# First attention of a hybrid network: group maxima taken a group ahead, a third stack buffer, and work laid out in pairs of slots

## The reference

```python
xn = (xg - mean) * jax.lax.rsqrt(var + EPS)
xn = xn.reshape(b, c, n) * norm_w[None, :, None] + norm_b[None, :, None]
qkv = jnp.einsum('oc,bcn->bon', qkv_w, xn) + qkv_b[None, :, None]
q, k, v = jnp.split(qkv, 3, axis=1)
...
attn = jnp.einsum('bhdn,bhdm->bhnm', q * scale, k * scale)
attn = jax.nn.softmax(attn, axis=-1)
out = jnp.einsum('bhnm,bhdm->bhdn', attn, v).reshape(b, c, n)
out = jnp.einsum('oc,bcn->bon', proj_w, out) + proj_b[None, :, None]
return out.reshape(b, c, h, w) + x_in
```

## Time and profile before

| | |
|---|---|
| median of 3 runs | 5458.73 us (5458.4 to 5465.98) |
| profiled execution | 5458.14 us, its span 5456.3 us |
| busy in the span | PE 4884.0 us (90%), DVE 3601.6 (66%), ACT 2986.6 (55%), POOL 1018.5 (19%) |
| mean granted clock of TensorE | 0.949 of 2.4 GHz |
| attention | from the start to about 2078 us |

### The profile page before, as it was taken

One profiled execution on the slowest core, in us unless ns is written; L12 is line 12 of the kernel. 1 busy time (PEld: TensorE's weight loads), 2 busy tenths in 40 slices (PEclk: granted clock), 3 DMA queues, 4 the chain that ended last, 5 costly groups with the idle time before them and its releaser, 6 DMA issues.

```text
span 5456.3 us, 90109 instructions
## 1 busy us (share of the span) xinstructions
PE 4884.0 (90%) x29729; PEld 2693.7 (49%) x29729; DVE 3601.6 (66%) x7699; ACT 2986.6 (55%) x5452; POOL 1018.5 (19%) x1348
## 2 busy tenths in 40 slices
PE   5999999999999988868888888889899999999999
PEld 1222222232222222247777777778755555555554
DVE  6777777777777744555656656555676766766765
ACT  2666666666666663315555555556655455555552
POOL 2221122232121222112333333333200000000000
PEclk7999999999999998879999999999999999999999
DMA  2522222232222211305454545454311111111112
GB/s 85 148 78 88 71 71 81 74 94 84 71 93 72 68 45 28 72 32 154 144 163 142 164 139 165 139 156 115 111 44 48 53 44 51 50 42 51 51 46 74
DMA packets 406330, 477.63 MB, mean 88 GB/s; under 512 B 87640, under 2 KB 249648, under 8 KB 403760
## 3 DMA queue, kind: packets, MB, share of 16 engines
q1 hardware_dynamic: 372128, 424.84, 25.8%
q0 software_dynamic: 20576, 35.55, 2.4%
q10 hardware_dynamic: 13168, 11.48, 0.8%
HBM read 308.54 MB, written 145.57 MB: 83 GB/s over the span
## 4 chain that ended last, share of the span: by engine, by line
PE 34%; DVE 16%; issue 3%; DVEq 3%; ACT 2%; ACTq 0%; SPq 0%; DMA 0%
PE n_ps_f L2157 4%; PE n_ps_f L2150 4%; PE n_ps_xy L1805 3%; PE n_ps_h L1795 3%; PE n_ps_c L2197 2%; PE n_ps_h L2209 2%; PE n_ps_f L2144 2%; PE n_ps_f L1653 2%; PE n_ps_xy L2213 1%; DVE n_stats L975 1%; PE n_ps_f L999 1%; DVE n_xln L987 1%; PE n_ps_h L2213 1%; DVEq L2029 1%; DVE n_down_weights L2028 1%
## 5 line engine op out<-in xcount | busy, mean ns | idle before, releaser
L600 ACT ACTIVATE a_probs<-ps_b 128x512 f32<-128x512 f32 x2048 | 1111.0, 594 | 734.9 <-PE ps_b L696 725.1
L456 DVE TENSOR_REDUCE a_negmax<-ps_a 128x1 f32<-128x1024 f32 x1024 | 1219.7, 1221 | 309.6 <-PE ps_a L640 301.1
L696 PE MATMUL ps_b<-a_q_stack,a_k_stack 99*128 99x512 bf16 x2048 | 651.7, 391 | 56.9 <-DMA a_q_stack<-a_shift 49.3
L640 PE MATMUL ps_a<-a_k_stack,a_q_stack 96*128 96x512 bf16 x2048 | 624.9, 403 | 74.3 <-DMA a_k_stack<-split_scratch 64.4
L710 PE MATMUL ps_o<-a_probs,a_v_ones 128*32 128x256 f32 x8192 | 670.5, 400 | 0.0
L1608 ACT ACTIVATE n_hidden<-n_ps_h,n_b 128x128 f32<-128x128 f32 x1472 | 419.3, 373 | 343.6 <-PE n_ps_h L1795 342.3
L1805 PE MATMUL n_ps_xy<-n_down_weights,n_hidden 128*128 x2944 | 409.7, 284 | 80.4 <-ACT n_xy L1622 74.2
L1805 PEld LDWEIGHTS n_ps_xy<-n_down_weights,n_hidden 128*128 128x128 f32 x2944 | 368.5, 196 | 118.2 <-issue 114.6
L2094 ACT ACTIVATE n_down_weights<-n_ps_h 128x512 f32<-128x512 f32 x288 | 172.1, 598 | 428.6 <-PE n_ps_h L2209 323.0
L1795 PE MATMUL n_ps_h<-n_xy,n_up_weights 128*128 128x128 f32 x2944 | 400.9, 280 | 4.5 <-issue 2.4
L696 PEld LDWEIGHTS ps_b<-a_q_stack,a_k_stack 99*128 99x128 bf16 x2048 | 201.0, 100 | 382.1 <-ACT a_probs L600 98.8
(11 more groups left out here) (346 smaller groups left out, 7655.8 us busy)
## 6 DMA issues: line engine op xcount, KB each, us to landing
n_up_weights<-in_L_ffn_W_dram SPq DMA_DIRECT2D x368, 256.0 KB
n_up_weights<-score_scratch SPq DMA_DIRECT2D x512, 128.0 KB, 2.9
split_scratch<-a_pieces SPq DMA_DIRECT2D x180, 256.0 KB
a_q_stack<-split_scratch SPq DMA_DIRECT2D x128, 192.0 KB, 3.6
a_k_stack<-split_scratch SPq DMA_DIRECT2D x128, 192.0 KB, 4.1
rows_scratch<-n_zero SPq DMA_DIRECT2D x16, 1472.0 KB, 10.0
outs_scratch<-n_xy SPq DMA_DIRECT2D x176, 128.0 KB, 2.0
n_xg<-rows_scratch SPq DMA_DIRECT2D x80, 256.0 KB, 3.2
```

What stands on the lines that cost most here:

```text
L456: dve.tensor_reduce(negmax[:, b, t:t + 1], bank, axis=AX.X, op=ALU.max, negate=True).then_inc(ring_read, 1)
L600: act.activation(probs[:, m % PROBS, 512 * k:512 * k + 512], ps_b[:, k, :], ACT.Exp).then_inc(b_exp, 1)
L640: last = pe.matmul(bank[:, cols], q_stack[0:KS, h, 128 * t:128 * t + 128], k_stack[0:KS, h, cols], start=True, stop=True)
L696: pe.matmul(ps_b[:, k, :], k_stack[:, h, 128 * t:128 * t + 128], q_stack[:, h, 512 * k:512 * k + 512], start=True, stop=True).then_inc(b_u ...
```

## The change

- **Order within pairs.** PE handles slots in pairs. In an even slot: shifted scores, then a half weighing of 512 columns. In an odd slot: shifted scores, then the ring entries, among them both maxima of the pair. Before, each slot had ring entries, shifted scores and a quarter weighing of 256 columns.
- **Maxima ahead.** Every pair has two maxima and no pair is without; the list runs 4 maxima further ahead of its group (`EARLIER`). The prologue computes these 4 more. The shifts come at slots 13, 29, 45, 61.
- **Third stack buffer.** The stacks of a group rotate over three places; the third lies in the part of `u_cols` that belongs to the last four images. These images' `u` goes to a DRAM scratch and is loaded back in three parts when the convolution begins.
- **Smaller parts.** Each piece of the maxima is sent as soon as it is ready; `project` is cut in two halves around the shifted scores of slot 31; ACT does its `take` and `qk` steps after the exponentials of the odd slot. The other steps move by some slots.

```diff
+        def stacks(i, g):
+
+            n = (G * i + g) % STACKS
+            return q_stacks[n], k_stacks[n]
...
         def normed():
 
-            work = [(0, ("moments",)), (1, ("sums", 0)), (1, ("norm",))]
-            return work + [(4, ("qk", 0)), (6, ("qk", 1)), (9, ("v",))]
+            work = [(1, ("moments",)), (3, ("sums", 0)), (3, ("norm",))]
+            return work + [(7, ("qk", 0)), (9, ("qk", 1)), (11, ("v",))]
 
         def projected():
 
-            return [(2, ("take", 1, 0)), (4, ("take", 1, 1)), (8, ("recip",)), (29, ("project",)), (30, ("moments2",)),
-                    (31, ("sums", 1)), (32, ("norm2",)), (34, ("turn2",))]
+            return [(1, ("take", 1, 0)), (3, ("take", 1, 1)), (10, ("recip",)), (30, ("project",)), (31, ("project_rest",)),
+                    (31, ("moments2",)), (35, ("sums", 1)), (35, ("norm2",)), (37, ("turn2",))]
 
         def maxima(ahead, g):
 
-            work = [(3 + n * 26 // QUAD, ("scores", ahead, g, n)) for n in range(QUAD)]
-            return work + [(18, ("shift", ahead, g, 0)), (30, ("shift", ahead, g, 1))]
+            return [("scores", ahead, g, n) for n in range(QUAD)]
+
+        EARLIER = 4
+
+        def all_maxima(front):
+
+            work = [(n // 2 * 2 + 1, w) for n, w in enumerate(maxima(0, 1)[EARLIER:])]
+            work += [(13, ("shift", 0, 1, 0)), (29, ("shift", 0, 1, 1))]
+            if front:
+                work += [(QUAD - EARLIER + n // 2 * 2 + 1, w) for n, w in enumerate(maxima(1, 0) + maxima(1, 1)[:EARLIER])]
+                work += [(45, ("shift", 1, 0, 0)), (61, ("shift", 1, 0, 1))]
+            return work
...
+                if G * i + g >= STACKS:
+                    sp.wait_ge(b_up, (G * i + g - STACKS + 1) * (2 * QUAD))
...
                     store_split(0, i + 1)
                     store_split(1, i + 1)
+                    load_stack(i + 1, 0)
                 send_shift(i, 1, 0)
                 send_shift(i, 1, 1)
                 if front:
-                    sp.wait_ge(b_up, i * (2 * SLOTS) + 2 * QUAD)
-                    load_stack(i + 1, 0)
+                    load_stack(i + 1, 1)
...
                 for m, works in enumerate(bodies[kind]):
+                    shifted_scores(i, m)
+                    if m % 2 == 0:
+                        if m >= J:
+                            weigh_values(i, m // J - 1, m % J // 2)
+                        elif kind != "first":
+                            weigh_values(i - 1, G * NT - 1, m % J // 2)
                     n = run(works, kind, i, n, table)
-                    shifted_scores(i, m)
-                    if m >= J:
-                        weigh_values(i, m // J - 1, m % J)
-                    elif kind != "first":
-                        weigh_values(i - 1, G * NT - 1, m % J)
...
+            for n, up in enumerate(late_in):
+                part = slice(PARTS[n], PARTS[n + 1])
+                sp.dma_start(u_cols[:, B - LATE:B, part, :].rearrange("p a c h -> p a (c h)"),
+                             u_dram[:, :, part, :].rearrange("a p c h -> p a (c h)")).then_inc(up, 16)
```

More of the change, by code:

```diff
@@ L192, in plan @@
         def plan(front, back):
             by_slot = [[] for _ in range(SLOTS)]
-            for s, work in (projected() if back else []) + (normed() if front else []) + maxima(0, 1):
+            for s, work in (projected() if back else []) + (normed() if front else []):
                 by_slot[s].append(work)
             for k in range(HALVES):
[L198 to L201, removed]
+                by_slot[QUAD + 1 + 2 * k].append(("take", 0, k))
@@ L202, in plan @@
+            for s, work in all_maxima(front):
+                by_slot[s].append(work)
             return by_slot
         RING = ("scores", "shift", "project", "sums", "qk", "v")
+        PE_ONLY = ("project_rest",)
         BY_ACT = ("qk",)
         ACT_WORK = BY_ACT + ("take",)
-        first = [work for _, work in normed()] + [("split",), ("rows",)] + [work for _, work in sorted(maxima(0, 0), key=lambda x: x[0])]
+        first = [work for _, work in normed()] + [("split",), ("rows",)] + maxima(0, 0)[:QUAD // 2] + [("shift", 0, 0, 0)] + maxima(0, 0)[QUAD // 2:]
@@ L208, in attention_phase @@
+        first += maxima(0, 1)[:EARLIER // 2] + [("shift", 0, 0, 1)] + maxima(0, 1)[EARLIER // 2:EARLIER]
         bodies = {"first": plan(True, False), "middle": plan(True, True), "last": plan(False, True)}
@@ L629, in _, with project_half @@
         def _(pe):
+            def project_half(bank, k):
+                cols = slice(512 * k, 512 * k + 512)
+                for g in range(G):
+                    last = pe.matmul(bank[:, cols], wproj[:, g, :], o_sums[:, g, cols], start=(g == 0), stop=(g == G - 1))
+                return last
             def step(work, i, nxt, prev, parity):
@@ L646, in step @@
                     pe.wait_ge(on_up, prev + 1)
-                    for k in range(HALVES):
-                        cols = slice(512 * k, 512 * k + 512)
-                        for g in range(G):
-                            last = pe.matmul(bank[:, cols], wproj[:, g, :], o_sums[:, g, cols], start=(g == 0), stop=(g == G - 1))
+                    project_half(bank, 0)
+                    return
+                elif what == "project_rest":
+                    last = project_half(bank, 1)
                 elif what == "sums":
@@ L685, in run @@
                         n += 1
+                    elif work[0] in PE_ONLY:
+                        step(work, i, nxt, i - 1 if kind != "closing" else B - 1, (odd + n - 1) % 2)
                 return n
```

98 lines of the change are left out of this document (54 added, 44 removed).

## The result

The changed kernel takes **5493.1 us** in the median of 5 runs (5484.35 to 5495.06), beside 5458.4 for the kernel before on the same chip: ratio **1.0061, 95% interval 1.0046 to 1.0075**. It is slower by more than the 0.2% that can be told from no change, and inside the predicted range; the predicted 5516 was 23 us too high. The profiled execution has a span of 5491.3 us, 35.0 more than the one of before.

A forecast was written before the change was run, and what follows sets the result against it. PE's instruction list was taken to set the pace. A middle image summed to 127.3 us against 122.5; 14 of them gave +67, the ends -10, so +57 on 5458.1: 5516 us, range 5410 to 5580.

The forecast's parts named there:

- PE's list without DVE waits: Middle image: 32 pairs of 2.86 us, 10.0 for other entries, 0.8 waiting for ACT; 102.3 us.
- shifts as third entries: Odd slots: a shift behind two maxima waits 1.1 us for a free bank; 4.3 us for four shifts.
- `qk`, `v` as third entries: Odd slots: the second maxima wait until ACT has read the bank; two `qk` and `v` lose 3.0 us.
- DVE at the image's start: Slots 63 to 5: PE's maxima wait while DVE does `moments`, `sums` and `norm`; 6.1 us lost.
- DVE behind `project`: Up to slot 39: PE's maxima wait while DVE does `moments2`, `norm2` and `turn2`; 8.6 us lost.
- work at the lower clock: Behind the idle at image start and `project`, PE's work runs at half speed: 1.5 us each, 3 an image.
- The pair: Two undisturbed slots: 2.86 us against 3.08 before, with a 512-column weighing of 1.01; ACT barely follows.
- The third rival: The wide weighing brings nothing, 1.14 us for 512 columns: 4.2 us an image, 5575 us; chance 0.05.
- rival 2: The lower clock at both places and the pairs behind costs 7 us an image instead of 3: 5572 us; chance 0.10.
- The DMA waits: PE's two waits at the image's start, 2.0 us, and later ones vanish; the next stacks' load stays hidden before slot 32.
- the ends: Prologue and first image 0, last image -9.5 and -4, convolution's first matmul 3 us later; together -10 us.
- Rival 1: Faster: clock holds (-3), PE's long entries absorb DVE's blocks and third entries (-4 an image): 5418 us; chance 0.22.

The follow-up runs named there:

- Experiments 3 and 5: 3: changed kernel with maxima spread over the slots as before, 5485.5 us; 5: changed kernel with quarter weighings of 256 columns again, 5666.3 us.
- Experiment 4: Changed kernel with the shift put ahead of the maxima in its slot: 5461.7 us, ratio 1.0015.
- experiment 2: One of three Newton steps in both group norms, in both kernels: changed kernel 5432.9 us (ratio 0.9962), kernel before 5447.7 us (0.9990).
- experiment 7: Experiment 4's kernel with the second group norm and its transpose cut into 12 portions over slots 35 to 57: 5374.6 us, ratio 0.9857.
- Experiment 8: The kernel of experiment 7 with the first group norm in three portions too and both `qk` in slot 9: 5362.1 us, ratio 0.9831.

## Why the prediction was right in sign and too high in size

The sum of a middle image, term by term, predicted and measured. A third entry's loss is measured from start to start: the shift starts 1.92 us behind the first maxima (626.29 to 628.21) where its turn is at 0.88, and the second maxima behind a `qk` 1.43 behind the first (735.85 to 737.28) where 0.44 is usual. The profile's 0.89 and 0.83 count only from the end of the matmuls before.

| Term | predicted us | measured us |
|---|---|---|
| PE's list without DVE waits | 102.3 | 101.8 |
| shifts as third entries | 4.3 | 3.4 |
| `qk`, `v` as third entries | 3.0 | 3.0 |
| DVE at the image's start | 6.1 | 5.3 |
| DVE behind `project` | 8.6 | 8.0 |
| work at the lower clock | 3 | 3.1 |
| sum | 127.3 | 124.6 (period 124.6) |

- **The pair.** 2.86 was predicted, 2.88 measured; the weighing of 1.01 measured 1.00. The third rival (1.14 for 512 columns) is out: 0.57 twice against 1.00 leaves 0.14 in each that doesn't depend on the columns. By the Trainium skill (TensorE: Matmul & The Clock Gate, section Back-to-back issue gap) it would have been close to nothing; the measurement decides, and for four weighings side by side the page's figure is too small. List: 32 x 2.88 = 92.2, and 9.6 for the other entries (two `qk` 3.4, `v` 1.8, `project` 3.5, the small ones 0.9). What I had wrong is what holds the pair: I made it PE's list with ACT barely behind. Experiments 3 and 5 show that ACT needs its two slots apart, and that in the new order the wide weighing is worth 0.44 a pair, 0.15 of it in the weighing itself.
- **Third entries.** The mechanism and the size of one were right: 1.04 us for a shift where I had 1.1, and 1.0 for a `qk` or `v`. The term of the shifts was too large because the one of slot 29 stood ahead of its maxima in the changed order, with 0.30 us. I had priced four equal shifts without looking at each one's place. Experiment 4 took 1.7 us an image of it away again.
- **The two zones.** 14.7 us from the first maxima of slot 63 where I had 15.4, and 20.2 from the end of `project` where I had 20.7. This was the core of the argument, DVE's blocks between reductions that PE can't run ahead of with two banks, and experiments 2 and 7 show it as the cause: shortened or cut up, it gives the time back; experiment 2 in the kernel before gives next to nothing.
- **The clock.** It fell at both places, but cost time at one. At the start it fell as the zone ended: 728.61 to 735.85 is 7.2 us for work of 0.44 + 0.53 + 1.00 + 0.44 + 1.72 = 4.1 at the upper level, 3.1 lost. Behind `project` the slow work lies inside the zone: 673.61 to 677.16 is 3.55 us for 1.97, but DVE had the second maxima of slot 37 read only at 677.41 (675.05 and 2.36), and PE wrote the second of slot 39 at 677.60, so a faster PE would have waited for it. I had 1.5 us at each place; that the total came out as 3 is luck. It is less than rival 2's 7.
- **The DMA waits** are gone, as predicted, and slot 32 didn't wait. How much the third buffer brought apart from the order wasn't tried alone. Experiment 8 shows how little slack the load has now: one pair.
- **The middle of the kernel and its ends** were wrong against each other. Measured on the two profiled executions: 13 middle periods (from the read at 248.97 on) +26.7 us, where my 4.8 an image would be 62; the ends +8.3, where I had -10. Of these, up to the read at 129.81 +10.3 (the step is one pair later, 2.9, and four more reductions, 4.7 by my estimate; the rest is open), the first image +1.8, so it gives nothing back; from the last `v` to the end -3.8. In this last part the way to the end of the last `project` is 9.8 us shorter, where I had 13.5, and only 0.9 of it lies between the first `project` of this image and the last weighings, where I had 9.5. Pairs without maxima don't run at ACT's 1.08 a slot but in 2.88 us, as this piece of PE's timeline of the changed kernel shows. In the kernel before, with a quarter weighing behind each shifted scores, they took 2.46 (the shifted scores at 2022.51, 2023.79 and 2024.97 on its timeline). The last line below is the convolution's first matmul of the changed kernel:

```profile
2047.21 0.61 PE L729 MATMUL ps_b<-a_q_stack,a_k_stack 99*128 99x512 bf16 x2
2048.29 0.88 PE L729 MATMUL ps_b<-a_q_stack,a_k_stack 99*128 99x512 bf16 x2 [0.47 <-ACT a_probs L622]
...
2050.09 0.60 PE L729 MATMUL ps_b<-a_q_stack,a_k_stack 99*128 99x512 bf16 x2
...
2109.41 10.86 PE L924 MATMUL c_ps_s<-u_cols,c_bands 128*128 128x512 f32 x20 [16.91 <-DMA u_cols<-u_scratch]
```

The convolution's first matmul came 1.7 us later behind the end of the last `project` than before (the earlier trace rows has the start of before), less than my 3, and all that follows took another 4.4 us more, which I had at nothing. That is not explained by any run.

So the mechanism held in its main terms, and the sign with it. The size did so less: a middle image lost 2.1 us and not 4.8, since nearly each term was a little too large, and that the total is no more than 23 us off owes to the ends, which were 18 us off the other way; that is luck. Rival 1 needed 4 us an image less than my sum, and it was 2.7 less.

## What to carry to other kernels

With a ring of two banks, the engine that fills it can't bridge a block of the reader that is longer than the slack of one round: PE's pair had 0.52 us of slack (2.88 less two reductions of 1.18), and the first norm's block of 5.2 us held it for 4.7 (waits of 0.75, 3.38 and 0.53). Leave such a block under slots that don't use the ring, or cut it into portions of about the slack and put one into each round; the latter brought 1.6% (experiment 4 to 7), moving the rounds' own work elsewhere cost as much as it gave. And spacing matters like length: an instruction that stands between two producers of the same bank pair can be worth more by its place than by its duration.

## What the runs showed of the hardware that I had not expected

- A granted clock of 0.50 came behind single waits of 3.2 and 3.4 us (with one of 0.5 behind each) and lasted 3.6 to about 7 us with PE busy. With waits of 0.24, 0.42 and 1.22 us at the image's start (experiment 8) it stayed at 1.00, and with the chain in portions (experiment 7) there is no slow row behind `project`. Yet in the kernel before it fell behind a wait of 1.19 us, so the length of one wait doesn't tell by itself.
- Four weighings side by side take 0.57 us for 256 columns and 1.00 for 512, so by these two 0.14 us of each group doesn't depend on the columns.
- A pair of shifted scores without any ring work takes 2.88 us with ACT busy 2.16 of it when the two scores start 1.08 us apart and a wide weighing follows one of them, and 2.46 us when a quarter weighing follows each and they start 1.18 to 1.28 us apart (kernel before).
